# The end of a fused kernel: the order of the last normalization, the gating and the products around it on three engine queues

## The chip, the core and the metric
The kernel is one program for one core of a Trainium2 chip. The metric is the device time of one execution in microseconds (us). The engines are named as in the profile: PE (matrix products and transposes), DVE (vector work), ACT (activations and copies), POOL, and SP, which only issues transfers here.

## The reference, cut to what matters
Four residual layers run over `x` of 8 x 128 rows of 512 numbers: attention, a mixture of experts, a second attention (32 heads), and an adapter layer. Each is `x = x + layer(layernorm(x))`. The change is in the last layer and where it meets the layer before it:

```python
h = xf @ gw1.T + gb1                         # 512 -> 32
h = relu(layernorm(h) * ln_gamma + ln_beta)
gates = h @ gw2.T + gb2                      # 8 adapters
top_v, top_i = top_k(gates, 2); top_g = softmax(top_v)
onehot = (top_i[..., None] == arange(8))
allowed = (onehot.sum(axis=0) <= capacity)   # counts over ALL 1024 rows
w = einsum('nke,nk,ke->ne', onehot, top_g, allowed)
main = xf @ weight.T                         # the dense product
tmp = einsum('ni,eir->enr', xf, lora_A) * w.T[:, :, None]
out = main + einsum('enr,ero->no', tmp, lora_B) / 16
```

The counts need the choice of every row, so no adapter product can be finished before the gating of the last rows is.

## The kernel before, in words
The 1024 rows are eight tiles of 128 rows (`x[:, b, :]`). They are worked on in two halves of four tiles. Every float32 product is made of three products of parts (`three`: high x high, high x low, low x high), so one "group" of 512 output columns over a depth of 512 is 12 matmuls of 512 columns. ACT writes the high part of an operand (`..._hi`), and DVE subtracts it from the source to give the low part (`..._lo`).

Each engine has a queue of its own, written out by hand, in order, and the engines meet at semaphores (`wait_ge`, `then_inc`). `vstep.step` makes DVE wait for its own instruction. PE's outputs go to eight PSUM banks: `score_banks` (0 to 3), `turn_banks` (4, 5) and `out_banks` (6, 7), each taken in turn; `banks.take` makes PE wait until the bank's last content has been read.

The second attention runs 32 steps for each half (`STEPS`). In the second half's steps 28 to 31 (`ending`) the first half's rows are normalized for the last layer (norm group 6) and that layer's weights are split into parts. Step 32 issues the product `h` of the gate for half 0 (`tensor_small(0, 0)`), step 33 the product `tmp` with `lora_A` and then the four transposes of `h` (`tensor_small(0, 1)`). The last addition of the attention to `x` (`vector_out`, line 2041) is at step 33.

A normalization of a half (group 7 is the second half of the last layer) has for each tile k: `norm_stats` (lines 403 and 404), one `norm_sqrt` on ACT for all four tiles (411), `norm_recip` (416), then `norm_scale` k (433, DVE), `norm_turn` k (442, four PE transposes), `norm_hi` k (453, ACT) and `norm_lo` k (460, DVE). The scaled tile lies in one of two buffers, so scale k waits for turn k - 2. `vector_norm(g, j)` and its like on ACT and PE do one slice j of this, so that a loop can spread the slices.

In step 31 DVE has, in this order, the low part of the attended rows (2019), the low part of the first half's last tile (460), the statistics of the second half's tiles 0 and 1, and then, as step 32, the two low parts `p1T_lo` of the turned softmax (1996), which PE's `tensor_attend(31)` (2008) multiplies next.

Behind the attention come `tensor_adapters`, `scalar_adapters` and `vector_adapters`. `dense(b)` is a dense product of tile b, which DVE adds to `x` (2381 before). For the tiles 4 to 7, `dense_open(b)` leaves the sum open in its bank, and the adapter product is added to it there. The gating of a half h is `vector_small(h, 1)` (the copy of the turned `h` from PSUM, 2251) and `vector_gating(h, 0)` to `(h, 4)`: 0 the statistics (2274 to 2278), 1 the normalization (2281 to 2289), 2 the gates (2291 to 2294), 3 the top two (1298 to 1304, 2298), 4 the softmax's end and the weights (2302 to 2306). ACT helps with a square root between 0 and 1 (`scalar_gating(h, 0)`, 2259) and an exponential between 3 and 4 (`scalar_gating(h, 3)`, 2262). When both halves are gated, DVE sums the choices (`chosen`, 2390), PE adds them over the rows (`counts`, 2340), DVE builds the weights `we` (2401), PE turns them (2347), DVE and ACT make `tw`, `la_hi` and `la_lo` (2406, 2374, 2409), and PE, DVE and SP do the adapter products (2358), the last additions (2413) and the stores tile by tile.

ACT holds one table of functions at a time. Square root and exponential are in different ones here, and an `ACT_TABLE_LOAD` stands in the queue where the function changes; the copies need none.

Of the kernel before, what the change touches and what calls it, by code (L numbers as in the profile page):

```python
# [14 lines left out]
P = 128  # L15
B = 8
# [108 lines left out]
def three(hi_lo_a, hi_lo_b):  # L125
    (ah, al), (bh, bl) = hi_lo_a, hi_lo_b
    return (ah, bh), (ah, bl), (al, bh)
# [38 lines left out]
def layers_kernel(nc, A, out):  # L166
    with ExitStack() as whole:
# [295 lines left out]
        def mm_group(ps, pairs):  # L463
            pairs = list(pairs)
            for n, (a, b) in enumerate(pairs):
                ins = nc.tensor.matmul(ps, a, b, start=(n == 0), stop=(n == len(pairs) - 1))  # L466
            return ins
# [1728 lines left out]
        def ending(i, weights, norm, norm_next, small):  # L2196
            if STEPS - 4 <= i < STEPS:
                norm(6, i - STEPS + 7)
                for n in range(2 * (i - STEPS + 4), min(2 * (i - STEPS + 4) + 2, KT + 2)):
                    weights(n)  # L2200
            if i == STEPS - 1:
                norm_next(7, 0)
            if i >= STEPS:
                small(0, i - STEPS)
# [3 lines left out]
                   lambda h, j: tensor_small(h, j))  # L2208

        def scalar_ending(i):  # L2210
            ending(i, scalar_adapter_weights, scalar_norm, scalar_norm, scalar_small)

        def vector_ending(i):
            ending(i, vector_adapter_weights, vector_norm, vector_norm, vector_small)

        def tensor_small(h, j):
            if j == 0:
                ps = banks.take(next(out_banks), ("h", h), (S["scT"], h + 3))
                pe.wait_ge(S["xn_ready"], HB * (7 + h))
                pe.wait_ge(S["w2_lo"], 1)  # L2220
                mm_group(ps[0:G1, :], [q for k in range(KT) for q in three(
                    (ws[0][:, k, P:SMALL], ws[1][:, k, P:SMALL]),
                    (xn1[h][0][:, k, :], xn1[h][1][:, k, :]))]).then_inc(S["gate_mm"], 1)
                return
            ps = banks.take(next(out_banks), ("tmp", h), (S["tmpT"], h + 1))
            mm_group(ps[:, :], [q for k in range(KT) for q in three(
                (ws[0][:, k, 0:P], ws[1][:, k, 0:P]),
                (xn1[h][0][:, k, :], xn1[h][1][:, k, :]))]).then_inc(S["tmp_mm"], 1)
            ps = banks.take(next(out_banks), ("h_t", h), (S["gate_sc"], h + 3))
            pe.wait_ge(S["scT"], h + 3)  # L2230
            for b in range(HB):
                ins = nc.tensor.transpose(ps[:, b * G1:(b + 1) * G1], hT[h][:, b * P:(b + 1) * P],
                                          ident[0:G1, 0:G1])
            ins.then_inc(S["gate_t"], 1)

        def scalar_small(h, j):
            if j == 0:
# [80 lines left out]
        def tensor_adapters():  # L2318
            def dense_open(b):
                ps = banks.take(next(score_banks), ("out", b), None)  # L2320
                pe.wait_ge(S["xn_ready"], HB * 8)
                for n, (a, c) in enumerate(dense_pairs(b)):
                    nc.tensor.matmul(ps[:, :], a, c, start=(n == 0), stop=False)

            for b in range(HB):
                if b >= 2:
                    norm_turn(7, b - 2, next(out_banks))
                ps = banks.take(next(score_banks), ("dense", b), (S["dense_add"], b + 1))
                pe.wait_ge(S["w2_lo"], KT + 1)
                mm_group(ps[:, :], dense_pairs(b)).then_inc(S["dense_mm"], 1)  # L2330
            for k in range(2, HB):
                norm_turn(7, k, next(out_banks))
            for j in range(2):
                tensor_small(1, j)
            for b in range(HB, B - 1):
                dense_open(b)
            ps = banks.take(next(turn_banks), "counts", (S["routed"], 2))
            pe.wait_ge(S["rank_consts"], RANK_CONSTS + 1)
            pe.wait_ge(S["taken"], 3)
            nc.tensor.matmul(ps[:, 0:TOP1 * E1], ones, chosen[:, :, :].rearrange("p k e -> p (k e)"),  # L2340
                             start=True, stop=True).then_inc(S["ranks"], 1)
            dense_open(B - 1)
            for h in range(2):
                ps = banks.take(next(turn_banks), ("we", h), (S["tw"], h + 1))
                pe.wait_ge(S["we"], h + 1)
                for b in range(HB):
                    ins = nc.tensor.transpose(ps[:, b * P:(b + 1) * P],
                                              we[h][:, b, :, :].rearrange("p e r -> p (e r)"), ident)
                ins.then_inc(S["we_t"], 1)
            for b in range(B):  # L2350
                if b < HB:
                    ps = banks.take(next(out_banks), ("out", b), (S["x_out"], b + 1))
                else:
                    ps = banks.of(("out", b))
                pe.wait_ge(S["la_lo"], b // HB + 1)
                pe.wait_ge(S["w2_lo"], KT + 2)
                for n, (a, c) in enumerate(lora_pairs(b)):
                    ins = nc.tensor.matmul(ps[:, :], a, c, start=(n == 0 and b < HB), stop=(n == 2))
                ins.then_inc(S["lora_mm"], 1)

        def scalar_adapters():
            for b in range(HB):
                scalar_norm(7, b + 1)
            for j in (5, 6):
                scalar_norm(7, j)
            for j in (0, 3):
                scalar_gating(0, j)
            for j in range(2):
                scalar_small(1, j)
            for j in (0, 3):  # L2370
                scalar_gating(1, j)
            for h in range(2):
                act.wait_ge(S["tw"], h + 1)
                nc.scalar.activation(la[h][0][:, :], tw[h][:, :], ACT.Copy).then_inc(S["la_hi"], 1)

        def vector_adapters():
            for b in range(HB):
                vector_norm(7, b + 1)
                dve.wait_ge(S["dense_mm"], b + 1)
                dve.wait_ge(S["y1_add"], 2 * STEPS)  # L2380
                TT(x[:, b, :], banks.of(("dense", b))[:, :], x[:, b, :], ALU.add).then_inc(S["dense_add"], 1)
            for j in (5, 6):
                vector_norm(7, j)
            for j in range(5):
                vector_gating(0, j)
            for j in range(2):
                vector_small(1, j)
            for j in range(5):
                vector_gating(1, j)
            TT_sum = nc.vector.tensor_reduce(chosen[:, :, :], goh[:, :, :, :].rearrange("p b k e -> p k e b"),  # L2390
                                             AX.X, ALU.add)
            TT_sum.then_inc(S["taken"], 1)
# [149 lines left out]
```

## Time and profile before
| what | us |
|---|---|
| runs of the kernel | 1236.09 median of 3 (1232.84 to 1236.33) |
| the profiled execution, its own time | 1236.35 |
| its span in the trace | 1235.0 |
| PE busy | 1185.1 (96% of the span) |
| DVE busy | 805.3 (65%) |
| ACT busy | 671.4 (54%) |
| POOL busy | 419.6 (34%) |

The span is from the first to the last instruction in the trace; the execution's own time has 1.35 us more. Shares are of the span. The last 50 us, from 1184.95 us on, are the adapter layer. A row of a timeline gives the start, the duration, the engine, the line and the tiles (written <- read), and in brackets the idle time of that engine before it and what ended it. Durations of neighbours overlap a little, so the distance of starts is the price of an instruction in a row of like ones.

### The profile page before, as it was taken

The page shows a single profiled execution, that of the slowest core. Times are in us where ns is not written, and L with a number is a line of the kernel's source. Part 1 is how long each engine was busy: PE and PEld are TensorE (multiplying, and loading weights), DVE is VectorE, ACT ScalarE, POOL GpSimd, SP SyncE. Part 2 cuts the span into 40 slices and gives each one's busy share as a digit, 9 for nine tenths or more (in the row PEclk, how much of TensorE's full clock was granted, in tenths as well). Part 3 has the DMA queues.
Part 4 walks back from the last instruction along what each step waited for, and adds up shares of the span by engine and source line. Part 5 has one row for each costly group of instructions (what it writes and reads, how often), then busy time and mean ns, then how long its engine had stood idle before and what let it go on. Part 6 is the DMA issues. An engine that isn't in the chain of part 4 may idle for free.

```text
span 1235.0 us, 16580 instructions
## 1 busy us (share of the span) xinstructions
PE 1185.1 (96%) x5948; PEld 913.7 (74%) x5948; DVE 805.3 (65%) x1511; ACT 671.4 (54%) x1562; POOL 419.6 (34%) x515
## 2 busy tenths in 40 slices
PE   8989999899999999799999999999999999999997
PEld 5646556577776777688888888877888888888765
DVE  3457777677766784756666567764566666677757
ACT  2245741577777883355555555643455555556621
POOL 2413434577777761022223232310122232322200
PEclk9999999999999999899999999999999999999999
DMA  8675422885788777221112122211221121221101
GB/s 290 173 172 133 155 77 102 300 205 103 153 212 248 155 143 190 71 57 60 60 44 68 43 62 67 61 52 53 70 63 46 44 68 60 61 68 27 59 1 68
DMA packets 72849, 127.93 MB, mean 104 GB/s; under 512 B 11640, under 2 KB 30968, under 8 KB 70072
## 3 DMA queue, kind: packets, MB, share of 16 engines
q1 hardware_dynamic: 53024, 73.90, 20.1%
q0 software_dynamic: 17296, 48.26, 15.7%
q10 hardware_dynamic: 2448, 4.72, 1.1%
q8 instruction: 47, 0.77, 0.3%
q14 instruction: 34, 0.28, 0.1%
HBM read 150.37 MB, written 26.48 MB: 143 GB/s over the span
## 4 chain that ended last, share of the span: by engine, by line
PE 82%; DVE 7%; DMA 5%; ACT 3%; issue 2%; SPq 0%; ACTq 0%; POOL 0%; POOLq 0%; DVEq 0%
PE bank L466 50%; PE bank L1220 11%; PE bank L2008 7%; PE bank L1984 4%; PE bank L679 2%; PE bank L693 2%; PE bank L1280 2%; PE bank L645 1%; PE bank L660 1%; PE bank L1241 1%; DMA wf_raw<-in_wffn,weight_row 1%; DMA q0st<-m0T 1%; DMA lb_raw<-in_lb 1%; DMA returned<-moe 1%; DMA q_rows<-q0T_lo 1%
## 5 line engine op out<-in xcount | busy, mean ns | idle before, releaser
L1976 POOL TENSOR_SCALAR p<-p,mx 128x256 f32<-128x256 f32 x256 | 162.8, 652 | 524.4 <-DVE mx L1970 524.4
L1187 DVE TENSOR_TENSOR wf_lo<-wf_raw,wf_hi 128x512 fp32r<-128x512 f32 x188 | 121.5, 688 | 33.8 <-ACT wf_hi L1181 29.1
L1962 ACT ACTIVATE p<-bank,mx 128x256 f32<-128x256 f32 x256 | 118.0, 485 | 10.7 <-DVE mx L1952 10.5
L466 PE MATMUL bank<-xnA_hi,w1q_hi 128*128 128x512 f32 x288 | 118.6, 412 | 3.6 <-DVE xnA_lo L460 3.2
L1181 ACT ACTIVATE wf_hi<-wf_raw 128x512 fp32r<-128x512 f32 x192 | 110.1, 625 | 9.4 <-DMA wf_raw<-in_wffn,weight_row 9.0
L466 PE MATMUL bank<-xnA_hi,w1q_lo 128*128 128x512 f32 x288 | 114.6, 398 | 0.0
L466 PE MATMUL bank<-xnA_lo,w1q_hi 128*128 128x512 f32 x288 | 114.1, 396 | 0.0
L1991 ACT ACTIVATE p1T_hi<-bank 128x512 fp32r<-128x512 f32 x128 | 75.1, 596 | 65.7 <-PE bank L1984 65.7
L1916 ACT ACTIVATE q1T_hi<-bank 128x512 fp32r<-128x512 f32 x64 | 38.2, 597 | 132.2 <-PE bank L466 132.2
L466 PE MATMUL bank<-w1o_hi,a1T_hi 128*128 128x512 f32 x256 | 105.2, 411 | 0.1
L466 PE MATMUL bank<-wf_raw,zT 128*128 128x512 f32 x220 | 102.9, 593 | 2.2 <-DVE x L1263 1.3
L1922 DVE TENSOR_TENSOR q1T_lo<-bank,q1T_hi 128x512 fp32r<-128x512 f32 x64 | 44.2, 691 | 93.0 <-ACT q1T_hi L1916 93.0
L466 PE MATMUL bank<-w1o_hi,a1T_lo 128*128 128x512 f32 x256 | 100.3, 392 | 0.0
L466 PE MATMUL bank<-w1o_lo,a1T_hi 128*128 128x512 f32 x256 | 100.2, 391 | 0.0
L1603 POOL DMA_INDIRECT moe<-ys,token_out x47 | 82.1, 1746 | 28.1 <-issue 12.5
L2041 DVE TENSOR_TENSOR x<-bank,x 128x512 f32<-128x512 f32 x64 | 44.2, 690 | 71.8 <-PE bank L466 71.6
L1996 DVE TENSOR_TENSOR p1T_lo<-bank,p1T_hi 128x512 fp32r<-128x512 f32 x128 | 86.2, 681 | 0.0
L1948 DVE TENSOR_REDUCE mx<-bank 128x2 f32<-128x512 f32 x128 | 81.5, 677 | 0.0
L1220 PE MATMUL bank<-wf_hi,xsT_hi 128*128 128x512 f32 x188 | 78.4, 417 | 1.1 <-DVE xsT_lo L1293 1.1
L1984 PE MATMUL bank<-consts,p 128*128 128x128 f32 x512 | 75.5, 273 | 2.1 <-DVE a1T_lo L2019 2.1
L1220 PE MATMUL bank<-wf_lo,xsT_hi 128*128 128x512 f32 x188 | 74.1, 394 | 0.0
L1582 POOL DMA_INDIRECT wf_raw<-in_wffn,weight_row x47 | 50.5, 1075 | 66.9 <-PE bank L466 29.1
(338 smaller groups left out, 2958.8 us busy)
## 6 DMA issues: line engine op xcount, KB each, us to landing
w_raw<-in_wq SPq DMA_DIRECT2D x64, 256.0 KB
w_raw<-in_wo SPq DMA_DIRECT2D x64, 256.0 KB
moe<-xn SPq DMA_DIRECT2D x2, 2304.0 KB, 11.7
returned<-moe SPq DMA_DIRECT2D x8, 512.0 KB, 7.8
q0st<-q_rows SPq DMA_DIRECT2D x14, 256.0 KB, 4.6
x<-in_x SPq DMA_DIRECT2D x8, 256.0 KB, 6.5
ctx<-in_ctxT SPq DMA_DIRECT2D x2, 1024.0 KB, 10.8
q_rows<-q0T_hi ACTq DMA_DIRECT2D x8, 256.0 KB
```

The lines of the kernel that those rows point to most:

```text
L466: ins = nc.tensor.matmul(ps, a, b, start=(n == 0), stop=(n == len(pairs) - 1))
L1181: nc.scalar.activation(wf[m % 2][0][:, a, c, :], raw[m % STREAMS][:, a, c, :], ACT.Copy).then_inc(S["gu_hi"], 1)
L1187: nc.vector.tensor_tensor(wf[m % 2][1][:, a, c, :], raw[m % STREAMS][:, a, c, :], wf[m % 2][0][:, a, c, :].bitcast(F32), ALU.subtract).the ...
L1220: ins = nc.tensor.matmul(ps[:, :], a, c, start=(k == 0 and t == 0), stop=(k == KT - 1 and t == 2))
L1603: nc.gpsimd.indirect_dma_start(out=moe[j % 2], out_offset=bass.IndirectOffsetOnAxis(ap=token_out[:, at:at + 1], axis=0), in_=ys[j % Y_RING ...
L1948: ins = nc.vector.tensor_reduce(m[:, 2 * n:2 * n + 2], banks.of(("s1", s, n))[:, :].rearrange("p (h k) -> p h k", h=2), AX.X, ALU.max)
L1962: ins = nc.scalar.activation(pr1[s % 2][:, h, :], banks.of(("s1", s, n))[:, hh * 2 * P:(hh + 1) * 2 * P], ACT.Exp, bias=m[:, UH + h:UH + h ...
L1976: ins = nc.gpsimd.tensor_scalar(pr1[s % 2][:, h, :], pr1[s % 2][:, h, :], m[:, 3 * UH + h:3 * UH + h + 1], 1.0, ALU.mult, ALU.mult)
L1984: ins = nc.tensor.transpose(ps[:, h * P:(h + 1) * P], pr1[s % 2][:, h, part * P:(part + 1) * P], ident)
L1991: nc.scalar.activation(p1T[0][:, part, :], banks.of(("t1", s, part))[:, :], ACT.Copy).then_inc(S["p1T_hi"], 1)
L1996: nc.vector.tensor_tensor(p1T[1][:, part, :], banks.of(("t1", s, part))[:, :], p1T[0][:, part, :].bitcast(F32), ALU.subtract).then_inc(S[" ...
L2008: ins = nc.tensor.matmul(ps[:, :], a, c, start=(part == 0 and n == 0), stop=(part == 1 and n == 2))
```

## The change
It reorders the three queues between the attention's last step and the first adapter product; no product is added or left out. (1) ACT takes a square root of a constant in step 31, between its part of the attention (`scalar_attend`, 2015) and the high part of the first half's last tile (`norm_hi(6, 3)`), and the real `norm_sqrt(7)` stands in step 33 ahead of the copy of `tmp`. (2) The statistics of the last two tiles are taken in steps 32 and 33. (3) Behind the attention, DVE scales, turns and splits the four tiles of norm 7 with the first half's gating between them; the turns use the turn banks. (4) The gate product of half 1 comes after `dense(1)`, its transposes after `dense(2)`, then `tmp`, then `dense(3)`; the second half's gating on DVE has the additions of the dense products between its parts. (5) `counts` comes behind two open dense products rather than three, the third follows it, and the last one stands behind the transposes of `we` rather than ahead of them.

```diff
--- before.py
+++ after.py
@@ -2208,10 +2208,18 @@
                    lambda h, j: tensor_small(h, j))
 
         def scalar_ending(i):
-            ending(i, scalar_adapter_weights, scalar_norm, scalar_norm, scalar_small)
+            if i == STEPS - 1:
+                nc.scalar.activation(hr[:, 0:1], eps, ACT.Sqrt)
+            if i == STEPS + 1:
+                norm_sqrt(7)
+            ending(i, scalar_adapter_weights, scalar_norm, nothing, scalar_small)
 
         def vector_ending(i):
-            ending(i, vector_adapter_weights, vector_norm, vector_norm, vector_small)
+            ending(i, vector_adapter_weights, vector_norm, vector_norm, nothing)
+            for k in (2, 3):
+                if i == STEPS + k - 2:
+                    dve.wait_ge(*norm_x_ready(7, k))
+                    norm_stats(7, k)
 
         def tensor_small(h, j):
             if j == 0:
@@ -2222,16 +2230,18 @@
                     (ws[0][:, k, P:SMALL], ws[1][:, k, P:SMALL]),
                     (xn1[h][0][:, k, :], xn1[h][1][:, k, :]))]).then_inc(S["gate_mm"], 1)
                 return
-            ps = banks.take(next(out_banks), ("tmp", h), (S["tmpT"], h + 1))
-            mm_group(ps[:, :], [q for k in range(KT) for q in three(
-                (ws[0][:, k, 0:P], ws[1][:, k, 0:P]),
-                (xn1[h][0][:, k, :], xn1[h][1][:, k, :]))]).then_inc(S["tmp_mm"], 1)
-            ps = banks.take(next(out_banks), ("h_t", h), (S["gate_sc"], h + 3))
-            pe.wait_ge(S["scT"], h + 3)
-            for b in range(HB):
-                ins = nc.tensor.transpose(ps[:, b * G1:(b + 1) * G1], hT[h][:, b * P:(b + 1) * P],
-                                          ident[0:G1, 0:G1])
-            ins.then_inc(S["gate_t"], 1)
+            if j == 1:
+                ps = banks.take(next(out_banks), ("tmp", h), (S["tmpT"], h + 1))
+                mm_group(ps[:, :], [q for k in range(KT) for q in three(
+                    (ws[0][:, k, 0:P], ws[1][:, k, 0:P]),
+                    (xn1[h][0][:, k, :], xn1[h][1][:, k, :]))]).then_inc(S["tmp_mm"], 1)
+            if j == 2 or h == 0:
+                ps = banks.take(next(out_banks), ("h_t", h), (S["gate_sc"], h + 3))
+                pe.wait_ge(S["scT"], h + 3)
+                for b in range(HB):
+                    ins = nc.tensor.transpose(ps[:, b * G1:(b + 1) * G1], hT[h][:, b * P:(b + 1) * P],
+                                              ident[0:G1, 0:G1])
+                ins.then_inc(S["gate_t"], 1)
 
         def scalar_small(h, j):
             if j == 0:
@@ -2322,24 +2332,28 @@
                 for n, (a, c) in enumerate(dense_pairs(b)):
                     nc.tensor.matmul(ps[:, :], a, c, start=(n == 0), stop=False)
 
-            for b in range(HB):
-                if b >= 2:
-                    norm_turn(7, b - 2, next(out_banks))
+            def dense(b):
                 ps = banks.take(next(score_banks), ("dense", b), (S["dense_add"], b + 1))
                 pe.wait_ge(S["w2_lo"], KT + 1)
                 mm_group(ps[:, :], dense_pairs(b)).then_inc(S["dense_mm"], 1)
-            for k in range(2, HB):
-                norm_turn(7, k, next(out_banks))
-            for j in range(2):
-                tensor_small(1, j)
-            for b in range(HB, B - 1):
+
+            for b in range(2):
+                for k in (2 * b, 2 * b + 1):
+                    norm_turn(7, k, next(turn_banks))
+                dense(b)
+            tensor_small(1, 0)
+            dense(2)
+            tensor_small(1, 2)
+            tensor_small(1, 1)
+            dense(3)
+            for b in range(HB, B - 2):
                 dense_open(b)
             ps = banks.take(next(turn_banks), "counts", (S["routed"], 2))
             pe.wait_ge(S["rank_consts"], RANK_CONSTS + 1)
             pe.wait_ge(S["taken"], 3)
             nc.tensor.matmul(ps[:, 0:TOP1 * E1], ones, chosen[:, :, :].rearrange("p k e -> p (k e)"),
                              start=True, stop=True).then_inc(S["ranks"], 1)
-            dense_open(B - 1)
+            dense_open(B - 2)
             for h in range(2):
                 ps = banks.take(next(turn_banks), ("we", h), (S["tw"], h + 1))
                 pe.wait_ge(S["we"], h + 1)
@@ -2347,6 +2361,7 @@
                     ins = nc.tensor.transpose(ps[:, b * P:(b + 1) * P],
                                               we[h][:, b, :, :].rearrange("p e r -> p (e r)"), ident)
                 ins.then_inc(S["we_t"], 1)
+            dense_open(B - 1)
             for b in range(B):
                 if b < HB:
                     ps = banks.take(next(out_banks), ("out", b), (S["x_out"], b + 1))
@@ -2359,34 +2374,53 @@
                 ins.then_inc(S["lora_mm"], 1)
 
         def scalar_adapters():
-            for b in range(HB):
-                scalar_norm(7, b + 1)
-            for j in (5, 6):
-                scalar_norm(7, j)
-            for j in (0, 3):
-                scalar_gating(0, j)
-            for j in range(2):
-                scalar_small(1, j)
-            for j in (0, 3):
-                scalar_gating(1, j)
+            name, value = norm_dest_free[7]
+            act.wait_ge(S[name], value)
+            norm_hi(7, 0)
+            norm_hi(7, 1)
+            scalar_gating(0, 0)
+            norm_hi(7, 2)
+            norm_hi(7, 3)
+            scalar_small(1, 0)
+            scalar_gating(1, 0)
+            scalar_gating(0, 3)
+            scalar_small(1, 1)
+            scalar_gating(1, 3)
             for h in range(2):
                 act.wait_ge(S["tw"], h + 1)
                 nc.scalar.activation(la[h][0][:, :], tw[h][:, :], ACT.Copy).then_inc(S["la_hi"], 1)
 
         def vector_adapters():
-            for b in range(HB):
-                vector_norm(7, b + 1)
+            def dense_add(b):
                 dve.wait_ge(S["dense_mm"], b + 1)
                 dve.wait_ge(S["y1_add"], 2 * STEPS)
                 TT(x[:, b, :], banks.of(("dense", b))[:, :], x[:, b, :], ALU.add).then_inc(S["dense_add"], 1)
-            for j in (5, 6):
-                vector_norm(7, j)
-            for j in range(5):
-                vector_gating(0, j)
-            for j in range(2):
-                vector_small(1, j)
-            for j in range(5):
-                vector_gating(1, j)
+
+            norm_recip(7)
+            norm_scale(7, 0)
+            norm_scale(7, 1)
+            vector_small(0, 1)
+            norm_scale(7, 2)
+            norm_lo(7, 0)
+            norm_lo(7, 1)
+            norm_scale(7, 3)
+            vector_gating(0, 0)
+            vector_gating(0, 1)
+            norm_lo(7, 2)
+            norm_lo(7, 3)
+            dense_add(0)
+            vector_gating(0, 2)
+            vector_gating(0, 3)
+            dense_add(1)
+            vector_small(1, 1)
+            vector_gating(1, 0)
+            dense_add(2)
+            vector_gating(1, 1)
+            vector_gating(0, 4)
+            vector_gating(1, 2)
+            vector_gating(1, 3)
+            dense_add(3)
+            vector_gating(1, 4)
             TT_sum = nc.vector.tensor_reduce(chosen[:, :, :], goh[:, :, :, :].rearrange("p b k e -> p k e b"),
                                              AX.X, ALU.add)
             TT_sum.then_inc(S["taken"], 1)
```

## Rows read from the trace of the kernel before

**Rows 1.** busy time by stretch of the ending (PEclk: granted clock, 1.00 full)
```profile
core 0: us, PE busy (x) PEld busy (x) DVE busy (x) ACT busy (x) POOL busy (x), PEclk, DMA share, GB/s
1184.95:1219.38 34.43, 29.40 (x129) 21.59 (x129) 25.11 (x96) 10.15 (x16) 0.00 (x0) 0.95 0.00 1
...
1200.65:1204.52 3.87, 3.87 (x10) 1.59 (x11) 3.30 (x16) 1.58 (x2) 0.00 (x0) 0.56 0.02 4
```

**Rows 2.** chain of waits, ending: start, us, what; three of its steps
```profile
1190.72 0.44 PE bank L442 x4
1191.16 2.80 PE bank L466 x12
...
1227.05 0.70 DVE x L2413
```

**Rows 3.** timeline of PE: start, us, instruction, [idle before <- releaser]
```profile
1174.81 0.39 PE L2008 MATMUL bank<-p1T_hi,v_hi 128*128 128x512 f32 x1
...
1184.52 0.43 PE L2232 MATMUL bank<-consts,hT 32*128 32x32 f32 x4
...
1200.65 0.40 PE L466 MATMUL bank<-xnB_hi,ws_hi 128*32 128x512 f32 x1 [1.50 <-DVE xnB_lo L460]
...
1219.38 0.37 PE L2340 MATMUL bank<-chosen,ones 128*128 128x16 f32 x2 [1.49 <-DVE chosen L2390]
1219.59 0.48 PE L2323 MATMUL bank<-wm_hi,xnB_hi 128*128 128x512 f32 x1
...
1222.43 1.03 PE L2347 MATMUL bank<-consts,we 128*128 128x128 f32 x8
1225.25 0.47 PE L2358 MATMUL bank<-lb_hi,la_hi 128*128 128x512 f32 x1 [1.78 <-issue]
```

**Rows 4.** timeline of DVE: last attention steps, norm of the second half
```profile
1171.42 0.68 DVE L460 TENSOR_TENSOR xnA_lo<-bank,xnA_hi 128x512 fp32r<-128x512 f32 x1
...
1173.63 1.25 DVE L1996 TENSOR_TENSOR p1T_lo<-bank,p1T_hi 128x512 fp32r<-128x512 f32 x2
...
1181.87 0.69 DVE L2041 TENSOR_TENSOR x<-bank,x 128x512 f32<-128x512 f32 x1 [4.18 <-PE bank L466]
...
1186.01 0.66 DVE L403 BATCH_NORM_STATS2 stats<-x 128x6 f32<-128x512 f32 x1
...
1197.23 0.69 DVE L2381 TENSOR_TENSOR x<-bank,x 128x512 f32<-128x512 f32 x1 [1.47 <-PE bank L466]
1197.84 0.54 DVE L433 TENSOR_SCALAR xn<-x,moments,rstd 128x512 f32<-128x512 f32 x1
```

**Rows 5.** timeline of DVE: gating of the second half of the rows
```profile
1209.60 0.29 DVE L2251 COPY h__244<-bank 128x128 f32<-128x128 f32 x1 [0.30 <-PE bank L2232]
1209.93 0.38 DVE L2274 BATCH_NORM_STATS2 hst<-h__244 128x6 f32<-128x32 f32 x3
...
1211.18 0.18 DVE L2281 RECIPROCAL hr<-hr 128x4 f32<-128x4 f32 x1 [0.36 <-ACT hr L2259]
...
1213.27 1.23 DVE L2291 TENSOR_TENSOR prod<-h__244,gw 128x1024 f32<-128x1024 f32 x1
...
1216.01 0.31 DVE L1298 MAX8 gmx<-gates 128x8 f32<-128x8 f32 x3
...
1218.00 0.16 DVE L2302 TENSOR_REDUCE gks<-gk 128x4 f32<-128x8 f32 x1 [0.28 <-ACT gk L2262]
...
1218.87 0.37 DVE L2390 TENSOR_REDUCE chosen<-goh 128x16 f32<-128x128 f32 x1
```

**Rows 6.** timeline of ACT
```profile
1170.19 0.60 ACT L2015 ACTIVATE a1T_hi<-bank 128x512 fp32r<-128x512 f32 x1 [3.24 <-PE bank L2008]
...
1186.92 0.30 ACT L411 ACTIVATE rstd<-moments,consts 128x4 f32<-128x4 f32 x1 [0.40 <-DVE moments L404]
...
1209.51 1.28 ACT L2259 ACT_TABLE_LOAD   x1
1210.85 0.30 ACT L2259 ACTIVATE hr<-hmv,consts 128x4 f32<-128x4 f32 x1
```

## Prediction

> **What bounds the kernel now.** I read the table of engines first: PE is busy for 96% of the span, so a change pays only where PE idles, or where work can be laid beside it. Then the stretches of the ending. From the last attention transposes to the counts PE idles 34.43 - 29.40 = 5.03 us, and over 3.87 us of that stretch the granted clock is 0.56, which means mostly the lower of its two levels [rows 1]. The chain of waits shows the rhythm of a turn of 0.44 us and a group of 12 matmuls of 2.80 us [rows 2]. The timeline of PE shows where it stands: 1.50 us before the second half's gate product, for the last low part of the norm, and 1.49 us before the counts, for DVE's `chosen` [rows 3]. The timeline of DVE shows why it is late: a tile is scaled only behind the addition of a dense product that PE had not finished (idle 1.47 us before line 2381) [rows 4], so the norm is spread over four dense products, and both gatings come after it. The second takes from 1209.60 to 1218.87 in one piece [rows 5], while PE has only open dense products to do. In that stretch DVE sets the end, and its work begins too late.
>
> So the number to forecast is C, the start of `counts`: 1219.38 now [rows 3]. What follows it takes 1235.0 - 1219.38 = 15.62 us.
>
> **PE's queue up to C.** I work it out with the attention as it runs now, and add what delays that at the end. It starts at 1184.52 with the first half's four transposes, which the change leaves there, and they take 0.44: 1184.96 [rows 2, 3]. Behind them stand four turns, the second half's four transposes (a form of the same pitch), and eight groups: dense 0 to 3, gate, `tmp`, and two open dense products. Before, there were nine groups up to C; one open product goes behind C. At 2.80 and 0.44 that is 8 x 2.80 + 5 x 0.44 = 24.60. The gate product counts at 2.80 too: before, it ran from 1200.65 at the low clock with ten matmuls in 3.87 us, against 2.33 for ten at the rhythm of a full group, so 1.5 us of the gain is that clock [rows 1, 2, 3]. Without waits C would be 1209.56.
>
> **Does DVE keep up? First the norm.** The last addition to `x` begins at 1181.87 and lasts 0.69: 1182.56 [rows 4]. One tile's statistics are left then, since the other's go into step 32, where DVE idles 4.18 us before that addition [rows 4]. From the start of such statistics to the start of the square root it takes 1186.92 - 1186.01 = 0.91, and the root 0.30 [rows 4, 6]: 1183.75. The reciprocal, 0.2 (0.18 [rows 5] and a step), gives 1183.95. The root itself goes ahead of the copy of `tmp` on ACT and delays nothing, for that copy waits for the product that ends right ahead of the transposes of 1184.52 [rows 3]. Two scales at a pitch of about 0.5 (0.54 lasting [rows 4]) end at 1184.95, so PE finds tile 0 ready at 1184.96, and tile 1. The copy of `h` (0.33 to the next start [rows 5]) ends at 1185.3. Scale 2 waits for turn 0 (1185.5) and ends at 1186.0; ACT's two high parts (0.60 lasting [rows 6]) end at 1186.1 and 1186.6; low parts 0 and 1 (0.61 apart, the pitch of 128x512 work, from 1197.23 to 1197.84 [rows 4]) and scale 3 end at 1187.85. PE does dense 0 until 1188.2 and wants scales 2 and 3 there, which are ready. The two turns end at 1189.1.
>
> **Then the gate product.** The first half's statistics of `h` and the root between them take 1211.18 - 1209.93 = 1.25, part 1 takes 1213.27 - 1211.18 = 2.09 [rows 5]: 1187.8 + 3.34 = 1191.15. ACT's high parts 2 and 3 are queued behind that root (1189.0) and end at 1190.2. Low parts 2 and 3 stand behind part 1 on DVE and end at 1192.4. PE ends dense 1 at 1184.96 + 4 x 0.44 + 2 x 2.80 = 1192.32. So the gate product waits 0.1. Below, this wait can be 0, with low parts early. Above I take what it is now, 1.50 [rows 3]. My value is 0.1, because every link of it has its own row. PE's C becomes 1209.66.
>
> **Then the gatings.** From 1192.4: addition 0.61; part 2 takes 1216.01 - 1213.27 = 2.74; part 3 takes 1218.00 - 1216.01 less the 0.28 of waiting for the exponential, 1.71 [rows 5]; addition 0.61: 1198.05. PE's gate, dense 2 and the transposes end at 1192.4 + 2.80 + 2.80 + 0.44 = 1198.45. ACT copies `hT` directly behind the gate product, well before those transposes; no exponential is ahead of it any more. From 1198.5: copy 0.33; statistics 0.88 (1.25 less 0.37 of waiting for the root [rows 5]); addition 0.61, which covers the root; part 1, 2.09; part 4 of the first half 0.87 (from 1218.00 to 1218.87); part 2, 2.74; part 3, 1.71; addition 0.61, which covers the exponential; part 4, 0.87 [rows 5]. The sum is 10.71: `chosen` starts at 1209.2 and `counts` 0.51 later, as now [rows 3, 5]: 1209.7. PE is there at 1209.66. Both queues come out together, so C is 1209.7, 9.7 us earlier. The additions cost DVE nothing more than now, where they stand ahead of the gating. The unknown is the order: about 20 instructions of 128x512 follow other neighbours than before, and if each cost 0.69 rather than 0.61, that is 1.6 us; 0 from below.
>
> **ACT's early table load** is the one part that costs. The root of a constant stands in step 31 behind the high part that runs at 1170.19 for 0.60, and ahead of the high part of the first half's last tile [rows 6]. The load is 1.28 and starts at 1170.81; the root begins 0.03 or more behind it and lasts between nothing and the 0.30 of the real one [rows 6]; I take 0.30, as the same function. So that tile's high part begins near 1172.3 and ends at 1172.9, and DVE's low part, now at 1171.42, begins near 1172.95: 1.5 later [rows 4]. DVE is full from there to `p1T_lo` (low part, two statistics, at 1173.63 the first of two), so these begin at 1175.15 and 1175.75 and end at 1175.85 and 1176.45 [rows 4]. PE wants the first at 1174.81 [rows 3] and gets it at 1175.9: PE waits 1.1, and its second three matmuls (1176.6) no more. What follows on PE follows this product, so all times from here on, C too, are later by 1.1. Below: 0.8, if the root of a constant lasts nothing.
>
> How long does a load hold ACT? This one's like starts at 1209.51 and ends at 1210.79, and the root starts at 1210.85, 0.06 behind it and 0.04 behind the end of the statistics that it waits for [rows 5, 6]. The Trainium skill (ScalarE: Activation LUTs, What ACT_TABLE_LOAD costs) gives 1.283 us for the load and about 1.38 more for a drain, 2.66 for each switch. By the row PE waits 1.1. By the page it would wait 2.5, and the sum would be 1.4 higher; the trace contradicts a drain behind the load. What the change gives back elsewhere is nothing: the load that stands now between the halves' roots falls away, but it ended before the statistics did.
>
> **Behind C.** The open dense product with its 12 matmuls, from C + 0.21, then the turned `we` from C + 3.05 [rows 3], as now. The last open product no longer stands ahead of them: it fills PE's 1.78 us of idle time before the first adapter product, which starts at C + 5.87 now and at C + 3.05 + 0.88 + 2.80 = C + 6.73 then [rows 3]. Its three matmuls end near C + 7.6. DVE begins the last additions at 1227.05 = C + 7.67 [rows 2], held by its own `la_lo`. So this costs nothing, with 0.1 us to spare; from above it is 0.86. SP's stores follow those additions. Bank waits: the open products 4 to 7 want additions 0 to 3; the last is done at 1208.3, before C. Turns 2 and 3 want low parts 0 and 1 (1187.4), before 1188.2.
>
> **Sum.** -9.7 + 1.1 = -8.6: C at 1210.8. 1236.35 - 8.6 = 1227.75 for the profiled execution, which lies 0.26 above the median of the runs: **1227.5 us**, -0.7%.
>
> **Rivals.**
> - *DVE falls behind.* The same mechanism, but DVE reaches C later by lost overlap (1.6) or the gate product waits its 1.5, up to 3.1 together. For it: there is no slack between the two queues at C. Against: each wait is covered by a neighbour. 1228.5 to 1230.6; chance 0.18.
> - *A table load holds ACT for twice its record.* Something as long as the load follows it, 1.3: the tile's high part ends at 1174.2, and PE waits 2.4 instead of 1.1: 1228.8. Against it stands the 0.06 of [rows 6]. Chance 0.06. The drain that the page on Activation LUTs in the Trainium skill describes would do about this.
> - *The early load is free*, since ACT starts it while it waits for PE ahead of 1170.19, where it idled 3.24 [rows 6]. For it: the idle time is there. Against: the load stands behind that high part in the queue. 1226.4; chance 0.08.
> - *The gain is given back after C.* The adapter products wait in a new order; it takes 6 us there to make it unmeasurable, and the rows give 0.86 at most. About 1234; chance 0.03.
> - *More than I count*: both queues are quicker by 1 us, as groups with no turn beside them save PE 0.05 each and the short DVE steps overlap more: 1226.5. No row speaks for it beyond the last digit. Chance 0.05.
> - *The other side: PE's clock.* If it were low over the whole of PE's new queue, the eight groups would cost nearly 0.43 a matmul (the rate in [rows 1]: 3.87 us for 10, of which part ran at full clock) rather than 0.233: 96 x 0.19 = 18 us, and the kernel would take 1245. It decides from 8.6 / 0.19 = 45 matmuls on. For it: the clock did fall in this stretch. Against: it fell right after PE had idled 1.50 us [rows 1, 3], and the new order has no such gap. Chance 0.02.
> - The forecast itself, within 1 us: 0.58.
>
> **Range and chances.** What can be told from no change is 0.3%, 3.7 us; the runs of before already span 3.5. The first rival reaches 1230.6; of it I take in all but the last 0.1. Below, a free load or faster groups reach 1226.4 or, with the spread of the runs (the lowest lies 3.2 below the median), a time near 1224. Range 1224.0 to 1230.5. Faster 0.94 (all but the given-back gain, the clock and some of the spread), same 0.04, slower 0.02.
>
> **What the profile after would show.** Right: an `ACT_TABLE_LOAD` near 1170.8, `p1T_lo` near 1175.2 and PE waiting 1.1 for it; `counts` 24.7 to 25.5 us behind the first half's transposes; PE busy nearly throughout between, granted clock 1.00; DVE idle only a few tenths; 15.6 us from `counts` to the end. Wrong: PE idle before line 2340 for `chosen`, or before the gate product for a low part by more than 0.5; `p1T_lo` at its old place, or PE waiting over 2 us for it; a clock under 1.00 past 1185; or a first last-addition later than 7.7 us behind `counts`.

## The result and the profile after

The changed kernel takes 1226.45 us (median of 13 runs, 1222.95 to 1231.97) against 1235.8 us (median of 13, 1232.84 to 1238.54) for the kernel before. The ratio is 0.9928, 95% interval 0.9915 to 0.9941, so it is faster, clear of the noise. Forecast were 1227.5 us and -8.6 us, a ratio of 0.9930.

The page of the profiled execution, its first line and part 1:

```profile
span 1225.8 us, 16579 instructions
...
PE 1181.9 (96%) x5948; PEld 913.5 (75%) x5948; DVE 804.5 (66%) x1511; ACT 669.3 (55%) x1561; POOL 418.9 (34%) x515
```

The span is 9.2 us shorter. To see where, I compare the starts of three instructions, the marks, in both traces: A, the start of `a1T_hi` in step 31 (1170.19 before [rows 6]); H, the first half's transposes of `h` (1184.52 [rows 3]); and C, the counts (1219.38 [rows 3]).

| stretch | before | after | difference | forecast |
|---|---|---|---|---|
| start to A | 1170.19 | 1169.54 | -0.65 | 0 |
| A to H | 14.33 | 15.43 | +1.10 | +1.1 |
| H to C | 34.86 | 25.32 | -9.54 | -9.7 |
| C to end | 15.62 | 15.51 | -0.11 | 0 |

The first line is no part of the change: the instructions up to A are the same, and A lay between 1167.45 and 1171.08 us in the eleven profiles of this study. Without it the marks give -8.55 us, against the forecast of -8.6. The timeline of ACT after, from A on:

```profile
1169.54 0.60 ACT L2015 ACTIVATE a1T_hi<-bank 128x512 fp32r<-128x512 f32 x1 [3.25 <-PE bank L2008]
1170.16 1.28 ACT L2212 ACT_TABLE_LOAD   x1
1171.45 0.20 ACT L2212 ACTIVATE hr<-consts 128x1 f32<-128x1 f32 x1
1171.56 0.58 ACT L453 ACTIVATE xnA_hi<-bank 128x512 fp32r<-128x512 f32 x1
1172.04 1.08 ACT L1991 ACTIVATE p1T_hi<-bank 128x512 fp32r<-128x512 f32 x2
...
1184.00 0.30 ACT L411 ACTIVATE rstd<-moments,consts 128x4 f32<-128x4 f32 x1 [3.71 <-DVE moments L404]
```

The table load starts 0.02 us behind the end of `a1T_hi`, the root of the constant 0.01 behind the load, and the last tile's high part begins 2.02 behind A. The real root (1184.00) needs no load. DVE:

```profile
1172.18 0.69 DVE L460 TENSOR_TENSOR xnA_lo<-bank,xnA_hi 128x512 fp32r<-128x512 f32 x1 [1.31 <-ACT xnA_hi L453]
...
1174.40 1.25 DVE L1996 TENSOR_TENSOR p1T_lo<-bank,p1T_hi 128x512 fp32r<-128x512 f32 x2
...
1186.03 0.55 DVE L433 TENSOR_SCALAR xn<-x,moments,rstd 128x512 f32<-128x512 f32 x1 [0.29 <-PE bank L442]
...
1191.65 1.29 DVE L460 TENSOR_TENSOR xnB_lo<-bank,xnB_hi 128x512 fp32r<-128x512 f32 x2
...
1199.21 0.29 DVE L2261 COPY h__244<-bank 128x128 f32<-128x128 f32 x1 [0.71 <-PE bank L2242]
...
1209.69 0.37 DVE L2424 TENSOR_REDUCE chosen<-goh 128x16 f32<-128x128 f32 x1
...
1217.89 1.28 DVE L2447 TENSOR_TENSOR x<-bank,x 128x512 f32<-128x512 f32 x2
```

The first rows show the delay handed on: the low part of line 460 is 2.64 us behind A (1.23 before [rows 4, 6]), and `p1T_lo` follows it as closely as before. At 1186.03 scale 2 waits 0.29 for PE's first turn. The row at 1191.65 has both low parts in one piece behind the gating, with no idle time. At 1199.21 DVE waits 0.71 us for PE, its longest wait between H and C. PE:

```profile
1175.11 0.50 PE L2008 MATMUL bank<-p1T_hi,v_hi 128*128 128x512 f32 x1 [0.76 <-DVE p1T_lo L1996]
...
1184.97 0.43 PE L2242 MATMUL bank<-consts,hT 32*128 32x32 f32 x4
...
1193.08 0.40 PE L466 MATMUL bank<-xnB_hi,ws_hi 128*32 128x512 f32 x1 [0.21 <-DVE xnB_lo L460]
...
1210.29 0.29 PE L2354 MATMUL bank<-chosen,ones 128*128 128x16 f32 x2
...
1213.26 1.03 PE L2361 MATMUL bank<-consts,we 128*128 128x128 f32 x8
...
1216.87 0.39 PE L2373 MATMUL bank<-lb_hi,la_hi 128*128 128x512 f32 x1
```

PE waits 0.76 us for `p1T_lo` (before, it came to this product at 1174.81, without a wait [rows 3]), 0.21 before the gate product where it was 1.50, and nothing before the counts, where it was 1.49. The stretches on both sides of the counts:

```profile
core 0: us, PE busy (x) PEld busy (x) DVE busy (x) ACT busy (x) POOL busy (x), PEclk, DMA share, GB/s
1184.97:1210.29 25.32, 25.11 (x122) 19.27 (x121) 22.44 (x91) 6.28 (x12) 0.00 (x0) 1.00 0.00 1
1210.29:1225.80 15.51, 12.47 (x59) 9.80 (x58) 9.73 (x16) 1.26 (x2) 0.00 (x0) 0.99 0.36 135
```

From H to C, PE is busy for 25.11 of 25.32 us with a granted clock of 1.00 (29.40 of 34.43 with 0.95 before [rows 1]).

### The profile page after: what moved, and what is told of

It is laid out like the page before. It is cut to its first block, busy times and chain, and to the rows that moved or that the text cites. A ratio compares the mean times of both kernels' runs of the same rounds, so it can differ in the third digit from the quotient of the medians.

```text
span 1225.8 us, 16579 instructions
## 1 busy us (share of the span) xinstructions
PE 1181.9 (96%) x5948; PEld 913.5 (75%) x5948; DVE 804.5 (66%) x1511; ACT 669.3 (55%) x1561; POOL 418.9 (34%) x515
## 4 chain that ended last, share of the span: by engine, by line
PE 80%; DVE 7%; DMA 5%; ACT 3%; issue 2%; POOL 1%; SPq 1%; ACTq 0%; POOLq 0%; DVEq 0%
PE bank L466 50%; PE bank L1220 10%; PE bank L2008 7%; PE bank L1984 4%; PE bank L679 2%; PE bank L693 2%; PE bank L1280 1%; PE bank L645 1%; DMA wf_raw<-in_wffn,weight_row 1%; PE bank L660 1%; PE bank L1241 1%; DMA x<-in_x 1%; DMA moe<-ys,token_out 1%; DMA q0st<-m0T 1%; PE bank L2333 1%
## 5 line engine op out<-in xcount | busy, mean ns | idle before, releaser
L1220 PE MATMUL bank<-wf_hi,xsT_lo 128*128 128x512 f32 x188 | 73.2, 389 | 0.0
```

What stands on the lines that cost most here:

```text
L1220: ins = nc.tensor.matmul(ps[:, :], a, c, start=(k == 0 and t == 0), stop=(k == KT - 1 and t == 2))
```

## The experiments

Times of whole executions vary by several us from the part ahead of A, so the differences of 1 us are read between the marks; the runs stand beside them. The changed kernel was run again beside the others (e0), to see how well the marks repeat.

> The changed kernel once more, beside the others of this call. Theory and rivals alike: 0.992 to 0.994 of the kernel before; from the last-but-one high part of the attention (a1T_hi of step 31) to the counts 40.75 us as in its first profile, against 49.19 in the kernel before.

Measured: 1227.28 us (median of 7), ratio 0.9945 (0.9926 to 0.9964). A to C took 40.72 us, where the first profile had 40.75, and C to the end 15.54. The marks repeat within 0.03 us, the ratios of the runs within 0.2%.

**The early root taken out (e1).**

```diff
-            if i == STEPS - 1:
-                nc.scalar.activation(hr[:, 0:1], eps, ACT.Sqrt)
             if i == STEPS + 1:
                 norm_sqrt(7)
```

> The changed kernel without the root of a constant in step 31. Theory (the table load there sits in the chain and costs PE 1.0 us): the load moves ahead of the real root of step 33, where ACT idles 3.71 us, PE no longer waits for p1T_lo, and from a1T_hi of step 31 to the counts it takes 39.7 us, 1.0 to 1.1 less than the changed kernel (about 1225.4 us). Rival (the early root is worth having, since a load in step 33 delays the norm): the norm's root is later, and the stretch is 40.75 or more.

Measured: 1225.02 us (median of 5), ratio 0.9925 (0.9906 to 0.9945). ACT's timeline has the load behind the copy `hT`:

```profile
1177.10 1.28 ACT L411 ACT_TABLE_LOAD   x1
1180.82 0.30 ACT L411 ACTIVATE rstd<-moments,consts 128x4 f32<-128x4 f32 x1 [2.43 <-DVE moments L404]
```

The load runs at once, and ACT then idles 2.43 us for the statistics. PE has its old place at `p1T_hi` and reaches the counts 39.65 us behind A (1167.45):

```profile
1172.08 0.39 PE L2008 MATMUL bank<-p1T_hi,v_hi 128*128 128x512 f32 x1
...
1207.10 0.29 PE L2352 MATMUL bank<-chosen,ones 128*128 128x16 f32 x2
```

That is 1.07 us less than with the early root, and H to C is unchanged at 25.31. The early root costs 1.1 us and gives nothing. In whole runs the two medians stand 2.3 us apart in that direction, but the intervals of the ratios overlap, so there the gain isn't resolved.

**The early root alone, in the kernel before (e2).**

```diff
         def scalar_ending(i):
+            if i == STEPS - 1:
+                nc.scalar.activation(hr[:, 0:1], eps, ACT.Sqrt)
             ending(i, scalar_adapter_weights, scalar_norm, scalar_norm, scalar_small)
```

> The kernel before with the root of a constant in step 31 and nothing else. Theory: p1T_lo is 1.4 later, PE waits about 1.0 for it, and from a1T_hi of step 31 to the counts it takes 50.2 us, 1.0 more than before (+0.08%). Rival (the delay is caught up by the waits on DVE further on, which end with PE's products): 49.2. Rival (the load holds ACT for twice its record): PE waits 2.3, 51.5.

Measured: 1235.45 us (median of 12), ratio 1.0011 (0.9997 to 1.0026). A (1167.78) to C took 50.29 us, 1.10 more than before, and A to H took 15.42 where it had taken 14.33, so all of it lies ahead of H:

```profile
1173.35 0.50 PE L2008 MATMUL bank<-p1T_hi,v_hi 128*128 128x512 f32 x1 [0.79 <-DVE p1T_lo L1996]
...
1218.07 0.37 PE L2342 MATMUL bank<-chosen,ones 128*128 128x16 f32 x2 [1.50 <-DVE chosen L2392]
```

Nothing later makes the delay good, and the load doesn't hold ACT for longer than its record.

**Three open products ahead of the counts (e3).**

```diff
-            for b in range(HB, B - 2):
+            for b in range(HB, B - 1):
                 dense_open(b)
...
-            dense_open(B - 2)
+            dense_open(B - 1)
...
-            dense_open(B - 1)
             for b in range(B):
```

> The changed kernel with the old tail: three open dense products ahead of the counts, the fourth between counts and the turned weights, none behind. Theory (PE's queue sets C, and the order behind C costs nothing): C is later by one group, 2.75 us, and from C to the end it takes 15.5 us as now; about +2.7 us against the changed kernel. Rival (DVE sets C by itself, and the last open product behind the turned weights delays the adapter products by 0.9): +1.9 us or less.

Measured: 1229.38 us (median of 8), ratio 0.9955 (0.9934 to 0.9977). A to C took 43.43 us, 2.71 more than in the repeated run, and C to the end 15.56. DVE was done long before PE came to the counts:

```profile
1207.63 0.37 DVE L2423 TENSOR_REDUCE chosen<-goh 128x16 f32<-128x128 f32 x1
```

```profile
1210.94 0.29 PE L2354 MATMUL bank<-chosen,ones 128*128 128x16 f32 x2
```

So in the new order a group less ahead of the counts is worth a whole group, and the group behind the turned `we` costs nothing. Beside the kernel before, this run shows what the rest of the change gives without the new tail: C comes 43.43 us behind A rather than 49.19, although the early root is in it. Of the 9.5 us from H to C, some 6.8 thus belong to the new order of the norm, the gating and the products, and 2.7 to the open product moved behind C. The parts (2) to (4) of the change were not run apart from each other.

**The gating behind the low parts (e4).**

```diff
             norm_scale(7, 3)
-            vector_gating(0, 0)
-            vector_gating(0, 1)
             norm_lo(7, 2)
             norm_lo(7, 3)
+            vector_gating(0, 0)
+            vector_gating(0, 1)
```

(On ACT, `scalar_gating(0, 0)` moves behind `norm_hi(7, 3)` to match.)

> The changed kernel with the first two parts of the first half's gating behind the low parts 2 and 3 of the norm instead of ahead of them (on DVE, and ACT's root behind its high parts to match). Theory (DVE has no slack at C, and the gating fills its wait for PE's turns 2 and 3): the gate product's wait of 0.2 us goes, but DVE idles 2 us before low part 2, of which 0.7 is made up in its idle time before the second copy of h; PE waits for the counts, C is 1.2 us later. Rival (PE alone sets C, DVE has slack): C within 0.3 us, and earlier rather than later.

Measured: 1227.68 us (median of 6), ratio 0.9942 (0.9926 to 0.9958). The gate product no longer waits, but DVE idles 1.91 us for the high part, and PE now idles for `chosen`:

```profile
1191.84 1.29 DVE L460 TENSOR_TENSOR xnB_lo<-bank,xnB_hi 128x512 fp32r<-128x512 f32 x2 [1.91 <-ACT xnB_hi L453]
...
1212.41 0.37 DVE L2424 TENSOR_REDUCE chosen<-goh 128x16 f32<-128x128 f32 x1
```

```profile
1212.92 0.36 PE L2354 MATMUL bank<-chosen,ones 128*128 128x16 f32 x2 [1.34 <-DVE chosen L2424]
```

A to C took 41.84 us, 1.12 more than in the repeated run. The whole runs don't resolve that. DVE had as good as no slack at C: what it loses beyond its wait of 0.71 is lost at the counts.

**The new order of the open products alone, in the kernel before (e5, and e8 with the clock kept).**

```diff
-            for b in range(HB, B - 1):
+            for b in range(HB, B - 2):
                 dense_open(b)
...
-            dense_open(B - 1)
+            dense_open(B - 2)
...
                 ins.then_inc(S["we_t"], 1)
+            dense_open(B - 1)
```

> The kernel before with only the new order of the open products (two ahead of the counts, one behind, the last behind the turned weights). Theory (before, DVE sets C and PE idles 1.5 us there): C stays at 49.2 us from a1T_hi of step 31 and 15.6 us follow it; no change in time, PE's idle time before the counts grows by 2.75 us. Rival (PE's order counts by itself): 1 to 2.7 us faster.

Measured: 1236.15 us (median of 12), ratio 1.0008 (0.9995 to 1.0022). A to C took 49.16 us, as before. But C to the end took 17.27, 1.65 more, which neither the theory nor the rival had. Windows and PE's timeline:

```profile
core 0: us, PE busy (x) PEld busy (x) DVE busy (x) ACT busy (x) POOL busy (x), PEclk, DMA share, GB/s
1219.83:1224.47 4.64, 4.64 (x15) 3.67 (x15) 1.76 (x4) 0.00 (x0) 0.00 (x0) 0.63 0.00 0
1219.83:1237.10 17.27, 14.13 (x58) 11.04 (x58) 9.73 (x16) 1.26 (x2) 0.00 (x0) 0.90 0.32 121
```

```profile
1219.83 0.36 PE L2340 MATMUL bank<-chosen,ones 128*128 128x16 f32 x2 [2.63 <-DVE chosen L2391]
...
1220.58 0.63 PE L2323 MATMUL bank<-wm_lo,xnB_hi 128*128 128x512 f32 x1
1221.00 0.63 PE L2323 MATMUL bank<-wm_hi,xnB_lo 128*128 128x512 f32 x1
...
1224.47 1.03 PE L2347 MATMUL bank<-consts,we 128*128 128x128 f32 x8
```

Behind 2.63 us of idle time the granted clock was 0.63 over the next group: eight of its matmuls are at the lower level and start some 0.43 apart rather than 0.23, and the turned `we` come 4.64 behind C rather than 3.05.

> The kernel before with the new order of the open products, as in e5, and eight more matmuls of 512 columns into a spare bank ahead of the counts, whose results are not used. Theory (what made e5's stretch from the counts to the end 17.27 us instead of 15.62 is the clock alone, which fell to 0.57 behind 2.63 us of idle time): the granted clock stays at 1.00 behind the counts, the stretch is 15.6 us and the time that of the kernel before. Rival (the last open product behind the turned weights delays the adapter products in the old order of things): 16.5 to 17.3 us with the clock at 1.00.

The edit puts eight more matmuls ahead of the counts:

```diff
+            spare = banks.take(next(turn_banks), "spare", (S["xn_ready"], 1))
+            for a, c in dense_pairs(0)[:8]:
+                nc.tensor.matmul(spare[:, :], a, c, start=True, stop=True)
             ps = banks.take(next(turn_banks), "counts", (S["routed"], 2))
```

Measured: 1234.85 us (median of 12), ratio 0.9991 (0.9978 to 1.0004).

```profile
core 0: us, PE busy (x) PEld busy (x) DVE busy (x) ACT busy (x) POOL busy (x), PEclk, DMA share, GB/s
1207.03:1213.31 6.28, 6.28 (x18) 4.96 (x19) 5.12 (x20) 3.29 (x4) 0.00 (x0) 0.50 0.00 1
1217.87:1233.40 15.53, 12.50 (x59) 9.80 (x57) 9.76 (x16) 1.26 (x2) 0.00 (x0) 1.00 0.36 135
```

C (1217.87) to the end took 15.53 us with the clock at 1.00, so the 1.65 were the clock. A to C was 49.73, 0.54 more than before. The clock was kept behind C only: ahead of it, behind 2.70 us of idle time before the second half's transposes of `h`, it was 0.50 over 6.28 us. So `chosen` begins 0.22 later from A (1217.04), and the added matmuls end behind it. The tail's new order by itself gives nothing, and with PE idle ahead of it, it can cost something.

**The clock kept up around the gate product, in the kernel before (e6).**

```diff
+            spare = banks.take(next(turn_banks), "spare", (S["xn_ready"], 1))
             for k in range(2, HB):
                 norm_turn(7, k, next(out_banks))
+                for a, c in dense_pairs(0)[:3 if k == 2 else 7]:
+                    nc.tensor.matmul(spare[:, :], a, c, start=True, stop=True)
```

> The kernel before with ten more matmuls of 512 columns into a spare bank, 3 behind the last-but-one turn of the norm and 7 behind the last, which fill PE's idle time there. Their results are not used. Theory (the low clock over the gate product, put at 1.5 us of the gain in the prediction, lies beside the first half's gating on DVE, and the copy hT waits for the exponential behind it): the granted clock stays 1.00, the gate product takes 2.8 instead of 4.3 us, and C does not move: no change in time. Rival (the clock was worth its 1.5 us): C 1.5 us earlier.

Measured: 1234.96 us (median of 12), ratio 1.0005 (0.9992 to 1.0017). The gate product runs from 1198.54 to 1201.30, 2.76 us at full clock, and C stays 49.18 us behind A (1168.07):

```profile
core 0: us, PE busy (x) PEld busy (x) DVE busy (x) ACT busy (x) POOL busy (x), PEclk, DMA share, GB/s
...
1198.54:1201.30 2.76, 2.76 (x14) 1.38 (x13) 2.26 (x14) 1.58 (x2) 0.00 (x0) 1.00 0.03 6
```

```profile
1206.12 0.21 ACT L2262 ACTIVATE gk<-gk 128x8 f32<-128x8 f32 x1 [5.30 <-DVE gk L2298]
1206.23 0.66 ACT L2240 ACTIVATE hT<-bank,gb 32x512 f32<-32x512 f32 x1
```

```profile
1217.25 0.37 PE L2343 MATMUL bank<-chosen,ones 128*128 128x16 f32 x2 [1.45 <-DVE chosen L2393]
```

ACT's rows show why. `hT` is copied behind the exponential of the first half's gating, which waits for DVE until 1206.12, 4.8 us after the gate product is done. The low clock in the kernel before cost nothing.

**Without the early root, and a tail cut finer (e7).** On top of the first experiment, the third open product is cut in two around the turned `we` of half 0, and the last one in two around the first two adapter products.

```diff
             for h in range(2):
+                dense_part(B - 2, h)
                 ps = banks.take(next(turn_banks), ("we", h), (S["tw"], h + 1))
...
-            dense_open(B - 1)
+            dense_part(B - 1, 0)
             for b in range(B):
+                if b == 2:
+                    dense_part(B - 1, 1)
```

> The changed kernel without the early root, and with the turned weights of half 0 after six matmuls of the third open product and those of half 1 behind it; the last open product is cut in two by the first two adapter products. Theory: DVE begins tw 1.4 us earlier behind C, PE's queue then sets the tail, C to the end 15.1 us instead of 15.5; together with the root 1.4 us less than the changed kernel, about 1225.0 us. Rival (the tail is held by SP's stores or by DVE's eight additions): 15.5 us as now.

Measured: 1225.39 us (median of 6), ratio 0.9923 (0.9906 to 0.9940). A to C took 39.61 us and C (1208.98) to the end 15.12:

```profile
1211.29 0.69 DVE L2448 TENSOR_TENSOR tw<-bank,tmpT 128x512 f32<-128x512 f32 x1
...
1217.92 4.09 DVE L2455 TENSOR_TENSOR x<-bank,x 128x512 f32<-128x512 f32 x6 [1.35 <-PE bank L2381]
```

DVE starts `tw` 2.31 us behind C (3.61 in the changed kernel), but then idles 1.35 for PE: the 1.30 shrink to 0.42 at the end, because PE now has no idle time behind C that could be filled. Between the marks this is the best version, 1.5 us less from A to the end than the changed kernel. In whole runs it can't be told from the version that only drops the early root.

## Why the prediction was right, point by point

- *DVE sets C before, since its work begins too late.* Shown. With PE relieved of one group there (e5), or run at full clock (e6), C did not move: 49.16 and 49.18 us behind A against 49.19.
- *PE's new queue: 24.60 us of work, waits 0.1.* Measured from H to C: 25.32, of which 0.21 is idle time. The other 25.11 stand against 25.04, the 24.60 and the 0.44 of the transposes at H. Counted from the same mark, the forecast was 1209.7 - 1184.52 = 25.18. The wait ahead of the gate product was 0.21 rather than 0.1: the low parts ended 0.1 later than summed (1192.94, where 1192.4 and H's own shift of 0.45 give 1192.85), and PE began 0.14 behind them.
- *Both queues meet at C.* Shown from both sides: a group more on PE costs 2.71 (e3), 1.91 us of idle time on DVE cost 1.12 (e4). That is its size less the 0.71 that DVE waits at the second copy of `h` and less the 0.09 by which DVE is ahead of PE at C (`counts` starts 0.60 behind `chosen`, and 0.51 where PE waits for it). The forecast had 0.45 for the wait at that copy; the difference is PE's later gate product. `chosen` began 24.72 us behind H, where 24.68 was forecast (1209.2 - 1184.52).
- *The early table load costs 1.1.* Measured 1.10 (A to H), and 1.10 again alone (e2), 1.07 back when taken out (e1). Its parts were off in opposite directions: the root of the constant lasted 0.20, not 0.30, so that PE came to its product 0.95 later, and the rest to H took 0.15 longer (9.86 against 9.71), as PE's first matmul behind a wait is followed 0.34 later, not 0.22.
- *What ACT waits behind a load.* The Trainium skill (ScalarE: Activation LUTs, What ACT_TABLE_LOAD costs) adds a drain of about 1.38 us to each switch. The trace disagrees: 0.01 us from the load's end to the root in the row at 1171.45, and 0.02 from the end of `a1T_hi` to the load. The rival that was built on a doubled load fell, and so did that of a free load.
- *The order behind C is free.* Shown by e3 (15.56 us against 15.54). The first last-addition began at 1217.89, 7.60 us behind C (7.67 before), though the first adapter product came at 1216.87, 6.58 behind C (5.87 before, 6.73 forecast). A clock under 1.00 past 1185 was named as a sign of being wrong. It shows only at the very end, 0.92 in the stretch from 1223.00 to 1225.80, where PE has no more work.
- *1.5 us of the gain is the clock.* Wrong as a share of the gain. The sum did not use it, as it went by PE's new queue and not by savings. But e6 shows that the low clock cost nothing before: that product had 4.8 us of cover behind it once the clock was full. What moved C is that DVE's queue is done earlier, with PE's queue short enough to be there too.
- *DVE falls behind by lost overlap, 0 to 1.6.* It lost none: the two low parts in the row at 1191.65 take 1.29 together, as the pair `p1T_lo` took 1.25 before [rows 4], and `chosen` came within 0.04 of the sum. That it came so close is luck: the second copy of `h` was 0.26 later than summed, and the stretch from it to `chosen` took 10.48 rather than 10.71.

## What to carry to other kernels

When two engines' queues alternate as the bound, write both out up to the point where they meet, with every wait in each. The later of the two sets the time, and an edit on the queue that waits there is worth nothing, as e5 and e6 show for PE in the kernel before. Once the queues come out together, either one sets the time, as e3 and e4 show. A table load that is pulled forward has to stand where ACT idles and behind everything that another engine waits for: here the load needed no help at all, since it ran by itself in the idle time ahead of its first user. A difference of 1 us in 1230 is seen between marks in the trace, not in the time of the whole.

## What was not expected of the hardware

The granted clock is not set by the length of one wait. In the kernel before, 1.50 us of idle time ahead of the gate product was followed by matmuls at the lower level [rows 1, 3]. The same wait in two other executions of the same order (e5 and e8, 1.50 us each, the edits being further on) was followed by a gate product at full clock, 2.76 and 2.77 us long. Idle times of 1.34 us (e4) and 1.49 (before) ahead of the counts left the clock at 1.00 behind them, and 2.63 us in e5 was followed by eight matmuls at the lower level.

Longer waits are no surer. Ahead of the second half's transposes of `h`, PE idled 2.69 us in e5, 2.70 in e8 and 2.68 in e6. Behind them the clock was 0.60 over 4.28 us in e5 and 0.50 over 6.28 us in e8, but 1.00 in e6. The windows, e5 first, then e6:

```profile
1209.52:1213.80 4.28, 4.28 (x14) 3.48 (x15) 3.36 (x19) 3.29 (x4) 0.00 (x0) 0.60 0.01 2
```

```profile
1206.95:1209.00 2.05, 2.05 (x11) 1.73 (x12) 1.37 (x10) 1.98 (x3) 0.00 (x0) 1.00 0.02 4
```

What else decides it stays open. For C the low clock in e5 cost nothing, since PE still waited 2.63 us there.
